# A transformer block with attention and routed experts on one core: GpSimd takes two elementwise steps from VectorE, its constants made between them

## The chip, the cores and the metric

The kernel runs on one core of a Trainium2 chip. The metric is the device time of one execution in microseconds (us). In the rows PE is TensorE (PEld its weight load), DVE is VectorE, ACT is ScalarE, POOL is GpSimd, SP is SyncE, which only issues DMAs; SPq and POOLq are the DMA-issuing sides of SP and POOL.

## What is computed

The input x holds 2 batches of 1024 tokens of 256 numbers. The result is x plus causal attention (16 heads of 16) plus a mixture of 8 experts (the 2 best for each token), both computed from the normalised rows:

```python
xn = _layernorm(x)
q, k, v = xn @ Wq + bq, xn @ Wk + bk, xn @ Wv + bv        # for each head
probs = softmax(causal(q @ k.T * HD ** -0.5))
attn = (probs @ v) @ Wo + bo
top, sel = top_k(xn @ Wr, 2);  w = softmax(top)
ffn = sum_e w_e * ((clip(silu(xn @ Wg[e]), -7, 7) * (xn @ Wu[e])) @ Wd[e])
out = x + attn + ffn
```

## The kernel before

Five instruction streams, one for each engine, walk one list, `PLAN`, made by `make_plan()`. Its entries are stages such as `("qk_lo", 3)`. Each engine has a table from stage names to its own functions (`walk`), skips the stages it has no function for, and executes the others strictly in the list's order. Semaphores tie the engines together, so a wait at the head of one engine's stream holds everything that stands behind it on that engine.

**Start.** Four quarters of 512 tokens: VectorE takes the variance (`"stats"`), GpSimd the inverse deviation (`inverse_deviation`, L555), VectorE normalises the rows (L743), TensorE transposes them (L936) and multiplies them by the q and k weights (L943).

**q and k in three parts.** The products are kept as a sum of three bf16 numbers, so that the scores can be made in bf16. For chunk k (128 x 512) ScalarE rounds the product and the bias to the first part (`qk_hi_part`, L640), VectorE subtracts it from the product (`qk_resid_part`, L752), ScalarE rounds the rest to the second part (`qk_mid_part`, L646), and VectorE subtracts again to get the third part (`qk_lo_part`, L760). SyncE stores each pair of chunks, 3 DMAs of 256 KB (`store`, L464), once all six parts are there, and loads the heads of a unit from the stored parts (`load`, L478). Chunks 0 to 7 (the first batch) are made at the start, chunks 8 to 15 (the second) in slots 0 to 24 of the main loop.

**GpSimd's constants.** Its stream begins with the masks, counters and ones that others need. One of them, `ones_row` (L572), is awaited by SyncE (`consts` at 4) before the DMA of ones into `packk` (L537), and behind that DMA stands all that SyncE issues later: the stores of the normalised rows (`store_xn`, L527), `store`, `load`.

**Routing.** VectorE finds the two best experts and a slot in the expert-sorted list for each token. GpSimd writes the list with 32 indirect DMAs, two for each group i of 128 tokens (`place_tokens(i)`, stage `"list"`, L595). SyncE loads the finished list (`load_list`, L505), VectorE makes token numbers of it (`token_of_slot`, L899 and L900), GpSimd gathers the rows (L604), and 39 expert tiles follow.

**Main loop.** 8 units of 4 heads in 12 steps g, each of 5 slots: four slots make scores and exponentials (TensorE L1028, ScalarE L668), the fifth multiplies by v (`weigh_v`, L1047). On diagonal steps GpSimd zeroes the upper triangle (`mask`, L620), and `weigh_v` waits for it. Beside them run the row maxima of the next unit (TensorE L1003, VectorE L788 and L791: a ring of three PSUM banks, so TensorE waits when VectorE stands still) and the experts' stages. The plan puts `("qk", 8 + k)` in slot 3k + 1 and `("qk_lo", 8 + k)` in slot 3k + 2 or one or two later, `("list", i)` for i of 4 and up at 2.5 slots each from slot 0, `("token",)` in slot 36, `("residual", t)` in slot 30 + 3t. The residual stage adds the output bias to x (`add_bias_to_x`, L775), 16 times 128 x 256; from slot 210 on others read its result.

Of the kernel before, what the change touches and what calls it, by code (L numbers as in the profile page):

```python
# [101 lines left out]
def stored(k, part):  # L102

    return part if qk_tile(k)[2] else PARTS - 1 - part
# [166 lines left out]
def build(nc, x_d, wqk_d, wvr_d, bqk_d, bv_d, wo_d, bo_d, wgu_d, wd_d, out_d):  # L271
    with ExitStack() as ctx:
# [272 lines left out]
        def _(pool):  # L545
# [7 lines left out]
            def inverse_deviation(q):  # L553
# [4 lines left out]
            pool.memset(padv[:, :], PAD).then_inc(consts, 1)  # L558
            chain(pool.memset(neghalf[:, :], -0.5))
            chain(pool.memset(ident[:, :], 0.0))  # L560
            chain(pool.affine_select(out=ident[:, :], in_=ident[:, :], compare_op=ALU.not_equal, fill=1.0, base=0,
                                     pattern=[[-1, P]], channel_multiplier=1))
            pool.tensor_copy(identb[:, :], ident[:, :]).then_inc(consts, 1)
            inverse_deviation(0)

            chain(pool.memset(maskrow[:, :], 0.0))
            pool.affine_select(out=maskrow[:, BANK - P:], in_=maskrow[:, BANK - P:], compare_op=ALU.is_ge, fill=NEG,
                               base=0, pattern=[[-1, P]], channel_multiplier=1).then_inc(consts, 1)
            inverse_deviation(1)
# [5 lines left out]
            chain(pool.memset(lower[:, :], 0.0))  # L575
            pool.affine_select(out=lower[:, :], in_=lower[:, :], compare_op=ALU.is_ge, fill=1.0, base=0,
                               pattern=[[-1, P]], channel_multiplier=1).then_inc(consts, 1)
            inverse_deviation(2)
            pool.memset(one8[:, :], 1.0)
            pool.iota(iota8[:, :], pattern=[[1, E]], base=0, channel_multiplier=0, allow_small_or_imprecise_dtypes=True)  # L580
            pool.iota(iota128[:, :], pattern=[[P, NT]], base=0, channel_multiplier=0,
                      allow_small_or_imprecise_dtypes=True)
            inverse_deviation(3)
# [136 lines left out]
        def _(dve):  # L720
# [450 lines left out]
```

## Time and profile before

| | before |
|---|---|
| median of 3 runs | 528.88 us (527.51 to 530.34) |
| the profiled execution, its own time | 527.32 us |
| its span, first to last instruction | 525.3 us |
| mean granted TensorE clock | 0.961 |
| busy: PE / DVE / ACT / POOL | 450.0 / 332.4 / 263.8 / 159.6 us |

The profile shows one execution. Busy time is the sum of an engine's instructions; what sets the end is better read from the chain of work that ended last, which names at each moment the instruction that the rest was waiting for. A granted clock of 1.0 is TensorE's 2.4 GHz, 0.5 is 1.2 GHz.

### The profile page before, as it was taken

The numbers are of one execution on the slowest core, as the hardware profiler recorded it, in microseconds if no ns is written. First come the engines' busy times: TensorE is split into PE (matmuls) and PEld (weight loads), VectorE is DVE, ScalarE is ACT, GpSimd is POOL, SyncE is SP. The second block draws the span as 40 slices with busy tenths as digits, with TensorE's granted clock in tenths as the row PEclk, the third lists the DMA queues.
The fourth block names the chain that finished last, engine by engine and source line by source line (L and its number), as shares of the span: only waits on it lengthen the run. The fifth ranks groups of instructions, "written<-read, shape, count | busy, mean of one in ns | idle before, by whom it ended". The sixth has DMA issues, their size and how long they took to land.

```text
span 525.3 us, 7823 instructions
## 1 busy us (share of the span) xinstructions
PE 450.0 (86%) x2368; PEld 203.5 (39%) x2368; DVE 332.4 (63%) x1023; ACT 263.8 (50%) x646; POOL 159.6 (30%) x198
## 2 busy tenths in 40 slices
PE   1777936987999999999989998899899989998876
PEld 1335612332344344434434444433433343433323
DVE  4585889785867686566665565546655666661671
ACT  1353300665446555564655454554555565656751
POOL 2210007584343233314341242123241333323020
PEclk9998965999799999999999999999999999999997
DMA  7469912587181008101810044001710101100851
GB/s 252 145 131 287 175 30 58 165 281 217 39 153 38 24 23 160 33 22 32 149 40 22 21 90 85 20 21 41 140 42 21 36 26 33 31 12 8 269 167 40
DMA packets 31726, 46.98 MB, mean 89 GB/s; under 512 B 6336, under 2 KB 18753, under 8 KB 31687
## 3 DMA queue, kind: packets, MB, share of 16 engines
q1 hardware_dynamic: 26055, 35.97, 27.9%
q0 software_dynamic: 4768, 9.33, 6.5%
q10 hardware_dynamic: 864, 1.19, 0.8%
q8 instruction: 20, 0.33, 0.3%
q14 instruction: 19, 0.16, 0.1%
HBM read 31.49 MB, written 15.63 MB: 90 GB/s over the span
## 4 chain that ended last, share of the span: by engine, by line
PE 65%; DVE 12%; ACT 7%; issue 6%; POOL 4%; DMA 4%; SPq 1%; POOLq 0%; ACTq 0%
PE ps_w L1085 14%; PE ps_y L1047 12%; PE ps_s L1028 9%; PE ps_s L1003 9%; PE ps_w L1113 7%; POOL slot_values L595 4%; ACT probs L668 4%; PE ps_w L1073 3%; PE ps_w L943 2%; DVE ps_s L788 2%; PE ps_w L967 2%; PE ps_w L1106 2%; DMA packk<-qk_parts 2%; PE ps_w L1080 1%; DVE mxa L791 1%
## 5 line engine op out<-in xcount | busy, mean ns | idle before, releaser
L668 ACT ACTIVATE probs<-ps_s 128x512 f32<-128x512 f32 (+3 forms) x384 | 176.9, 495 | 113.3 <-PE ps_s L1028 112.2
L788 DVE CUSTOM_DVE_ANT_0 ps_s<-ps_s,maskrow 128x128 f32<-128x128 f32 (+3 forms) x256 | 124.7, 500 | 59.6 <-PE ps_s L1003 58.6
L1003 PE MATMUL ps_s<-packk,packq 96*128 96x512 bf16 (+3 forms) x384 | 125.7, 344 | 18.6 <-DVE mxa L791 10.4
L1028 PE MATMUL ps_s<-packq,packk 99*128 99x512 bf16 (+3 forms) x384 | 121.4, 334 | 6.8 <-ACT probs L668 5.2
L791 DVE TENSOR_REDUCE mxa<-ps_s 128x1 f32<-128x512 f32 x128 | 88.2, 689 | 55.9 <-PE ps_s L1003 54.5
L1085 PE MATMUL ps_w<-wgu,xgt 128*128 x156 | 82.8, 613 | 3.3 <-issue 2.0
L1047 PE MATMUL ps_y<-probs,v 128*32 128x512 f32 (+3 forms) x768 | 82.7, 502 | 2.3 <-ACT probs L668 1.6
L610 POOL DMA_INDIRECT expert_rows<-yo,slots x39 | 39.6, 1015 | 125.7 <-ACT yo L706 123.4
L620 POOL TENSOR_SCALAR_AFFINE_SELECT probs<-probs 128x512 f32<-128x512 f32 x64 | 41.9, 654 | 112.0 <-ACT probs L668 111.6
L1028 PEld LDWEIGHTS ps_s<-packq,packk 99*128 99x128 bf16 x384 | 36.6, 98 | 91.6 <-ACT probs L668 55.0
L1003 PEld LDWEIGHTS ps_s<-packk,packq 96*128 96x128 bf16 x384 | 38.3, 100 | 64.0 <-issue 19.3
L604 POOL DMA_INDIRECT xg<-xn_rows,token x39 | 37.9, 972 | 34.6 <-PE ps_w L1080 23.0
L595 POOL DMA_INDIRECT slot_values<-slot_val,pos x32 | 32.1, 1002 | 53.0 <-DVE pos L884 44.1
L1113 PE MATMUL ps_w<-xnt,hidt 128*128 x156 | 41.6, 389 | 2.9 <-DVE y L821 2.4
L943 PE MATMUL ps_w<-xnt,wqk 128*128 128x512 f32 x64 | 33.8, 646 | 3.3 <-ACT xnt L630 1.9
L1085 PEld LDWEIGHTS ps_w<-wgu,xgt 128*128 128x128 f32 x156 | 25.8, 189 | 21.6 <-issue 18.4
L1113 PEld LDWEIGHTS ps_w<-xnt,hidt 128*128 128x128 f32 x156 | 27.8, 189 | 12.2 <-issue 7.4
L694 ACT ACTIVATE tanh<-ps_w 128x256 f32<-128x256 f32 x39 | 15.0, 384 | 33.9 <-PE ps_w L1085 33.9
L1047 PEld LDWEIGHTS ps_y<-probs,v 128*32 128x32 f32 x768 | 15.3, 108 | 39.8 <-ACT probs L668 22.3
L706 ACT ACTIVATE yo<-ps_w 128x256 f32<-128x256 f32 x39 | 15.0, 384 | 27.0 <-PE ps_w L1113 27.0
L907 DVE SCALAR_TENSOR_TENSOR tanh<-tanh,ps_w 128x256 f32<-128x256 f32 x39 | 16.2, 416 | 11.0 <-ACT tanh L694 10.9
L1073 PE MATMUL ps_w<-wo,yt 128*128 128x256 f32 x64 | 19.4, 429 | 4.3 <-ACT yt L681 2.3
(107 smaller groups left out, 395.0 us busy)
## 6 DMA issues: line engine op xcount, KB each, us to landing
qk_parts<-stage SPq DMA_DIRECT2D x24, 256.0 KB, 3.4
wgu<-in_wgu SPq DMA_DIRECT2D x8, 512.0 KB
stage<-expert_rows SPq DMA_DIRECT2D x16, 256.0 KB, 3.8
packq<-qk_parts SPq DMA_DIRECT2D x8, 384.0 KB, 5.3
packk<-qk_parts SPq DMA_DIRECT2D x8, 384.0 KB, 7.2
x<-in_x SPq DMA_DIRECT2D x4, 512.0 KB, 8.5
xn_rows<-probs SPq DMA_DIRECT2D x4, 512.0 KB, 9.2
packq<-qk_parts SPq DMA_DIRECT2D x8, 256.0 KB, 7.9
```

Of the source, the lines that this page charges most:

```text
L595: pool.indirect_dma_start(out=slot_d, out_offset=bass.IndirectOffsetOnAxis(ap=pos[:, k, i:i + 1], axis=0), in_=slot_val[:, i, k:k + 1], in ...
L610: pool.indirect_dma_start(out=z_d, out_offset=bass.IndirectOffsetOnAxis(ap=slots[:, i:i + 1], axis=0), in_=yo[:, i % 2, :], in_offset=None ...
L620: pool.affine_select(out=cols, in_=cols, compare_op=ALU.is_ge, fill=0.0, base=0, pattern=[[0, UH], [1, P]], channel_multiplier=-1).then_in ...
L668: act.activation(probs[:, g % 2, h, 0:width], ps_s[:, score_bank(k), 0:width], ACT.Exp, scale=SCALE)\
L788: ins = dve.tensor_tensor_reduce(out=chunk, in0=chunk, in1=maskrow[:, BANK - width:], scale=1.0, scalar=NEG, op0=ALU.add, op1=ALU.max, acc ...
L791: ins = dve.tensor_reduce(into, chunk, op=ALU.max, axis=AX.X)
L943: return pe.matmul(ps_w[:, bank, :], wqk[:, op, c, P * grp:P * (grp + 1)], xnt_moe[:, c, cols], start=c == 0, stop=c == DC - 1)
L1003: pe.matmul(ps_s[:, SCORE_RING + n % NAT_RING, 0:width], packq[0:MAXROW, u % SLOTS, h, P * i:P * (i + 1)], packk[0:MAXROW, u % SLOTS, h, B ...
L1028: pe.matmul(ps_s[:, score_bank(k), 0:width], packk[0:KROWS, u % SLOTS, h, P * j:P * (j + 1)], packq[0:KROWS, u % SLOTS, h, t0:t0 + width], ...
L1047: ins = pe.matmul(ps_y[32 * h:32 * h + 32, t0 - BANK * c:BANK], v[:, TB * b + j, at:at + 32], probs[:, g % 2, h, 0:width], start=j == 0, s ...
L1085: return pe.matmul(ps_w[:, bank, :], xgt[:, i % 2, c, :], wgu[:, bass.ds(expert[i] * (DC * 2 * F) + c * 2 * F, 2 * F)], start=c == 0, stop ...
L1113: ins = pe.matmul(ps_w[:, bank, 0:D], hidt[:, i % 2, c, :], wd[:, bass.ds(expert[i] * (DC * D) + c * D, D)], start=c == 0, stop=c == DC - 1)
```

## The change

`qk_lo_part` and `add_bias_to_x` move from VectorE's table to GpSimd's, at the same places of the plan. GpSimd's constants, so far written in one piece ahead of its walk, are cut in four functions that are called at the stages `("stats", 0)` to `("stats", 3)`. In the third, the memset of `ones_row` also waits for `qk_lo` at 2.

```diff
-            pool.wait_ge(rstd_ready, 2)
-            pool.memset(ones_row[MAXROW:KROWS, :], 1.0).then_inc(consts, 1)
-            pool.wait_ge(consts, 4)
...
+            def triangle():
+
+                pool.wait_ge(rstd_ready, 2)
+                pool.wait_ge(qk_lo, 2)
+                pool.memset(ones_row[MAXROW:KROWS, :], 1.0).then_inc(consts, 1)
+                pool.wait_ge(consts, 4)
...
+            def prepare(q):
+                (first_constants, mask_and_ones, triangle, counters)[q]()
...
-            walk({"list": place_tokens, "gather": gather, "scatter": scatter, "s": mask})
+            def qk_lo_part(k):
+                w, op = divmod(k, 2)
+                cols = slice(BANK * op, BANK * (op + 1))
+                pool.wait_ge(qk_mid, k + 1)
+                pool.tensor_tensor(stage[:, w % 2, stored(k, 2), cols], resid[:, k % 2, :], stage[:, w % 2, stored(k, 1), cols],
+                                  ALU.subtract).then_inc(qk_lo, 1)
+
+            def add_bias_to_x(t):
+                wait_freed(pool, ("bias",))
+                pool.tensor_tensor(x[:, t, :], x[:, t, :], bo[:, :], ALU.add).then_inc(residual_ready, 1)
+
+            walk({"stats": prepare, "qk_lo": qk_lo_part, "residual": add_bias_to_x, "list": place_tokens, "gather": gather,
+                  "scatter": scatter, "s": mask})
...
-            def qk_lo_part(k):
-                w, op = divmod(k, 2)
-                cols = slice(BANK * op, BANK * (op + 1))
-                dve.wait_ge(qk_mid, k + 1)
-                dve.tensor_tensor(stage[:, w % 2, stored(k, 2), cols], resid[:, k % 2, :], stage[:, w % 2, stored(k, 1), cols],
-                                  ALU.subtract).then_inc(qk_lo, 1)
...
-            def add_bias_to_x(t):
-                wait_freed(dve, ("bias",))
-                dve.tensor_tensor(x[:, t, :], x[:, t, :], bo[:, :], ALU.add).then_inc(residual_ready, 1)
```

**GpSimd's order at the start, of before.** The stream from the second inverse deviation (`rstd`) on; the memset of `wgu` is `ones_row`.

```order
L555 TENSOR_TENSOR rstd<-vareps,neghalf 128x4 [waits var_ready]
L572 MEMSET wgu 3x1024 [waits rstd_ready]
L575 MEMSET lower 128x128 [waits consts]
L576 AFFINE_SELECT lower<-lower 128x128 [waits const_step]
L555 TENSOR_TENSOR rstd<-vareps,neghalf 128x4 [waits var_ready]
```

The same place, of the changed kernel.

```order
L555 TENSOR_TENSOR rstd<-vareps,neghalf 128x4 [waits var_ready]
L638 TENSOR_TENSOR stage<-resid,stage 128x512 [waits qk_mid] x2
L579 MEMSET wgu 3x1024 [waits qk_lo,rstd_ready]
L581 MEMSET lower 128x128 [waits consts]
L582 AFFINE_SELECT lower<-lower 128x128 [waits const_step]
L555 TENSOR_TENSOR rstd<-vareps,neghalf 128x4 [waits var_ready]
L638 TENSOR_TENSOR stage<-resid,stage 128x512 [waits qk_mid] x2
```

Two third parts now stand ahead of `ones_row`, and two more behind the third inverse deviation.

**GpSimd's order in slots 0 to 40 of the main loop, of before.** The DMAs to `slot_values` write the list, AFFINE_SELECT is the mask of one step, the DMAs to `xg` are the first gathers.

```order
L595 DMA slot_values<-slot_val,pos 4992x1 [waits list_init,pos_ready]
L595 DMA slot_values<-slot_val,pos 4992x1 x11
L620 AFFINE_SELECT probs<-probs 128x4x128 [waits probs_ready]
L595 DMA slot_values<-slot_val,pos 4992x1 x4
L620 AFFINE_SELECT probs<-probs 128x4x128 [waits probs_ready]
L595 DMA slot_values<-slot_val,pos 4992x1 x4
L620 AFFINE_SELECT probs<-probs 128x4x128 [waits probs_ready]
L595 DMA slot_values<-slot_val,pos 4992x1 x4
L620 AFFINE_SELECT probs<-probs 128x4x128 [waits probs_ready]
L595 DMA slot_values<-slot_val,pos 4992x1 x8
L604 DMA xg<-xn_rows,token 128x256 [waits xn_out,token_ready]
```

The same place, of the changed kernel, up to the third mask; behind it four more third parts stand among the last 12 list DMAs, and three bias additions behind the last of these.

```order
L606 DMA slot_values<-slot_val,pos 4992x1 [waits list_init,pos_ready]
L606 DMA slot_values<-slot_val,pos 4992x1 x9
L638 TENSOR_TENSOR stage<-resid,stage 128x512 [waits qk_mid]
L606 DMA slot_values<-slot_val,pos 4992x1 x2
L631 AFFINE_SELECT probs<-probs 128x4x128 [waits probs_ready]
L638 TENSOR_TENSOR stage<-resid,stage 128x512 [waits qk_mid]
L606 DMA slot_values<-slot_val,pos 4992x1 x4
L631 AFFINE_SELECT probs<-probs 128x4x128 [waits probs_ready]
L638 TENSOR_TENSOR stage<-resid,stage 128x512 [waits qk_mid]
L606 DMA slot_values<-slot_val,pos 4992x1 x2
L638 TENSOR_TENSOR stage<-resid,stage 128x512 [waits qk_mid]
L606 DMA slot_values<-slot_val,pos 4992x1 x2
```

Eight third parts now stand between the tenth list DMA and the last, the first of them ahead of the first mask.

## Rows read from the trace of the kernel before

**Rows 1.** The page, chain that ended last: its shares by engine.

```profile
PE 65%; DVE 12%; ACT 7%; issue 6%; POOL 4%; DMA 4%; SPq 1%; POOLq 0%; ACTq 0%
```

**Rows 2.** The chain in order of time, start: start us, us, what.

```profile
28.54 0.70 DVE stage L760
...
30.36 2.62 DMA qk_parts<-stage
...
35.34 9.58 DMA packk<-qk_parts
```

**Rows 3.** Timeline of SP's DMA issues, start: start us, us, instruction.

```profile
15.08 0.94 SPq L537 DMA_DIRECT2D packk<-wgu  x1
...
16.51 3.74 SPq L527 DMA_DIRECT2D xn_rows<-probs  x1
...
22.43 8.43 SPq L464 DMA_DIRECT2D qk_parts<-stage  x6
```

**Rows 4.** Windows: us, busy of PE PEld DVE ACT POOL, PEclk, DMA share, GB/s.

```profile
18.50:21.00 2.50, 1.51 (x7) 0.53 (x5) 1.55 (x3) 1.23 (x4) 0.00 (x0) 1.00 0.26 46
...
31.00:32.00 1.00, 1.00 (x4) 0.52 (x3) 0.93 (x8) 0.00 (x0) 0.00 (x0) 1.00 1.01 340
```

**Rows 5.** Timeline of ScalarE and GpSimd, start, and ScalarE at chunk 8.

```profile
20.06 0.61 ACT L646 CAST stage<-resid 128x512 bf16<-128x512 f32 x1
20.98 0.62 ACT L646 CAST stage<-resid 128x512 bf16<-128x512 f32 x1 [0.31 <-DVE resid L752]
...
14.11 0.95 POOL L572 MEMSET wgu<- 3x1024 bf16 x1
...
95.43 0.62 ACT L646 CAST stage<-resid 128x512 bf16<-128x512 f32 x1 [0.33 <-DVE resid L752]
```

**Rows 6.** Instruction groups of POOL and DVE: busy, mean ns, idle before.

```profile
L620 POOL TENSOR_SCALAR_AFFINE_SELECT probs<-probs 128x512 f32<-128x512 f32 x64 | 41.9, 654 | 112.0 <-ACT probs L668 111.6
...
L561 POOL TENSOR_SCALAR_AFFINE_SELECT ident<-ident 128x128 f32<-128x128 f32 x1 | 0.3, 286 | 0.2 <-POOL ident L560 0.2
...
L760 DVE TENSOR_TENSOR stage<-resid,stage 128x512 bf16<-128x512 f32 x16 | 11.5, 723 | 2.5 <-ACT stage L646 1.9
...
L775 DVE TENSOR_TENSOR x<-x,bo 128x256 f32<-128x256 f32 x16 | 6.9, 431 | 0.0
```

**Rows 7.** The chain in order of time, end of the list.

```profile
124.13 4.08 DMA slot_values<-slot_val,pos
128.22 1.79 DMA slots<-slot_values
...
130.25 0.18 DVE token L900
```

**Rows 8.** Timeline of GpSimd among the list DMAs, and its wait behind them.

```profile
91.90 0.96 POOL L595 DMA_INDIRECT slot_values<-slot_val,pos  x1 [0.30 <-issue]
96.62 0.65 POOL L620 TENSOR_SCALAR_AFFINE_SELECT probs<-probs 128x512 f32<-128x512 f32 x1 [3.76 <-ACT probs L668]
...
108.61 1.23 POOL L595 DMA_INDIRECT slot_values<-slot_val,pos  x1 [0.17 <-issue]
...
117.62 1.16 POOL L595 DMA_INDIRECT slot_values<-slot_val,pos  x1 [0.30 <-issue]
...
130.71 0.98 POOL L604 DMA_INDIRECT xg<-xn_rows,token  x1 [5.62 <-DVE token L900]
```

**Rows 9.** Timeline of VectorE beside the first of these long list DMAs.

```profile
108.05 0.95 DVE L760 TENSOR_TENSOR stage<-resid,stage 128x512 bf16<-128x512 f32 x1 [0.68 <-ACT stage L646]
```

**Rows 10.** Waits from 126 to 135 us: who waited for whom, us, times, longest.

```profile
PE ps_s L1003 <- DVE mxa L788: 3.3, 1, 3.3
```

**Rows 11.** Timeline of SP, the experts' down weights.

```profile
119.63 3.83 SPq L501 DMA_DIRECT2D xnt<-in_wd  x6
```

**Rows 12.** The chain in order of time, a bias addition in it.

```profile
143.38 0.28 DVE x L775
```

**Rows 13.** Window behind the wait for the list, columns as in rows 4.

```profile
130.00:140.00 10.00, 8.85 (x37) 2.66 (x38) 7.72 (x26) 3.71 (x8) 4.15 (x5) 0.66 0.25 71
```

More of the change, by code:

```diff
@@ L556, in inverse_deviation @@
                     .then_inc(rstd_ready, 1)
[L558 to L569, printed above, removed]
-            pool.wait_ge(rstd_ready, 2)
-            pool.memset(ones_row[MAXROW:KROWS, :], 1.0).then_inc(consts, 1)
-            pool.wait_ge(consts, 4)
-            chain(pool.memset(lower[:, :], 0.0))
@@ L576, in _ @@
[L576 to L582, printed above, removed]
@@ L583, in _, with first_constants @@
-            inverse_deviation(3)
-            pool.iota(iota_t[:, :], pattern=[[1, MAX_TILES]], base=0, channel_multiplier=0,
-                      allow_small_or_imprecise_dtypes=True)
-            pool.iota(slot_val[:, :, :], pattern=[[2 * P, NT], [1, 2]], base=0, channel_multiplier=2).then_inc(consts, 1)
-            pool.memset(ones[:, :], 1.0).then_inc(consts, 1)
+            def first_constants():
+                pool.memset(padv[:, :], PAD).then_inc(consts, 1)
+                chain(pool.memset(neghalf[:, :], -0.5))
+                chain(pool.memset(ident[:, :], 0.0))
+                chain(pool.affine_select(out=ident[:, :], in_=ident[:, :], compare_op=ALU.not_equal, fill=1.0, base=0,
+                                         pattern=[[-1, P]], channel_multiplier=1))
+                pool.tensor_copy(identb[:, :], ident[:, :]).then_inc(consts, 1)
+                inverse_deviation(0)
@@ new lines, in mask_and_ones @@
+            def mask_and_ones():
+                chain(pool.memset(maskrow[:, :], 0.0))
+                pool.affine_select(out=maskrow[:, BANK - P:], in_=maskrow[:, BANK - P:], compare_op=ALU.is_ge, fill=NEG,
+                                   base=0, pattern=[[-1, P]], channel_multiplier=1).then_inc(consts, 1)
+                inverse_deviation(1)
+            def triangle():
[3 more added lines that the diff above has]
+                pool.wait_ge(consts, 4)
+                chain(pool.memset(lower[:, :], 0.0))
+                pool.affine_select(out=lower[:, :], in_=lower[:, :], compare_op=ALU.is_ge, fill=1.0, base=0,
+                                   pattern=[[-1, P]], channel_multiplier=1).then_inc(consts, 1)
+                inverse_deviation(2)
@@ new lines, in counters @@
+            def counters():
+                pool.memset(one8[:, :], 1.0)
+                pool.iota(iota8[:, :], pattern=[[1, E]], base=0, channel_multiplier=0, allow_small_or_imprecise_dtypes=True)
+                pool.iota(iota128[:, :], pattern=[[P, NT]], base=0, channel_multiplier=0,
+                          allow_small_or_imprecise_dtypes=True)
+                inverse_deviation(3)
+                pool.iota(iota_t[:, :], pattern=[[1, MAX_TILES]], base=0, channel_multiplier=0,
+                          allow_small_or_imprecise_dtypes=True)
+                pool.iota(slot_val[:, :, :], pattern=[[2 * P, NT], [1, 2]], base=0, channel_multiplier=2).then_inc(consts, 1)
+                pool.memset(ones[:, :], 1.0).then_inc(consts, 1)
@@ L918, in first_constants @@
                     widen_v_bias()
-            walk({"stats": variance, "ln": normalise_rows, "qk": qk_resid_part, "qk_lo": qk_lo_part,
+            walk({"stats": variance, "ln": normalise_rows, "qk": qk_resid_part,
                   "store": first_constants, "top": best_two, "place": place_slots, "token": token_of_slot,
-                  "bias": add_bias, "residual": add_bias_to_x, "nat": row_max, "negate": negate_max, "neg": copy_neg,
+                  "bias": add_bias, "nat": row_max, "negate": negate_max, "neg": copy_neg,
                   "norm": normalise, "moe_hid": hidden, "sum": add_experts, "proj": add_projection})
```

## The prediction, made before the changed kernel had run

> **What bounds the kernel now.** I read first the chain that ended last, by engine: TensorE has 65% of it, VectorE 12%, GpSimd only 4% [rows 1]. So work taken from VectorE is worth little on the average, and the question is where the chain runs through the work that changes hands or through GpSimd. The chain in order of time answers it: there are two such places.
>
> The first is the start. The chain passes the third part of chunk 3 on VectorE (28.54 to 29.24), the store behind it (last DMA issued at 30.36, landed at 32.98) and the load of the first heads (landed at 44.92) [rows 2]; TensorE has nothing to do before that load is in. The second is the list. Its last DMA starts at 124.13 and lands 4.08 us later, the list is loaded in 1.79, and the token numbers are made at 130.25 [rows 7]. VectorE waits for the list in its own stream, so its row maxima stop, and TensorE stands idle for 3.3 us behind them [rows 10]. Ahead of this GpSimd runs from 96.62 to the end of the list with no wait longer than the gaps of about 0.3 us between its DMAs [rows 8]: what is added to its stream there arrives later at everybody.
>
> **What GpSimd needs for a third part.** No row shows a GpSimd subtraction of this size. From below, its mask reads one input of 128 x 512 f32 and takes 654 ns; its 128 x 128 form takes 286 [rows 6]. So 384 more elements cost 368 ns, 0.96 ns each, over a fixed 0.16 us. From above I take twice the mask, 1.31 us, as two inputs of that size must pass. I choose t = 0.16 + 2 x 512 x 0.00096 = 1.15 us, near the upper end because the operation does read two tensors; VectorE needs 0.72 [rows 6]. A bias addition, half as long, comes to 0.65 us by the same sum, against 0.43 on VectorE.
>
> **The change at the start.** The second parts of chunks 0 and 1 end at 20.67 and 21.60 [rows 5], so the third parts on GpSimd run 20.7 to 21.9 and 21.9 to 23.05; VectorE had them done before the store was issued at 22.43 [rows 3]. The store itself would be 0.7 us late. But `ones_row` now waits for both: 0.95 us of memset [rows 5] brings it to 24.1, and SyncE stands at that wait with everything behind it. Its DMA of ones was issued at 15.08, so it moves by 9.0 us, and the two stores of normalised rows, which used to go out in a gap, move with it. The second of these took 3.74 us to issue, until 20.25 [rows 3], and the 16 DMA engines were only 26% busy, at 46 GB/s, while it stood there [rows 4]. I read that as the slow little DMA of ones in front of it, and it keeps its place in front. Issuing of ones and rows took 20.25 - 15.08 = 5.17 us, so SyncE comes to the first store at 24.1 + 5.17 = 29.3 instead of 22.43, 6.9 us late. The second store could not go before 29.24 in the old order either, so the loss is mostly made up; what is left is data. At 340 GB/s [rows 4] the second 512 KB of rows need 1.5 us and the two stores (six times 256 KB) 4.6 us. From 29.3 plus about 0.9 us until data flows and is confirmed that gives 36.3, against 32.98: **+3.3 us**. The load of 9.58 us behind it starts as much later, and TensorE, idle already, waits as much longer. The bounds: 0.7 us, if the long issue was not due to the ones (then only the slower third parts are seen), and 6.9 us, if the second store keeps its distance from the first. VectorE's own relief here buys nothing, since the chain passes it once, and GpSimd takes over exactly that piece.
>
> **The change in the list.** The first third part of the second batch, chunk 8, can't start before its second part is ready, at 95.43 + 0.62 = 96.05 [rows 5]. Before, GpSimd filled that time with list DMAs 11 and 12 (90.64 to 92.86: 0.96, a gap of 0.30, 0.96) and then waited 3.76 us for the exponentials [rows 8]. Now it waits with only ten done, runs the third part, then the two DMAs (2.22 us), and comes to the first mask at 96.05 + 0.1 + t + 0.2 + 2.2 = 99.7 for t = 1.15, where it was at 96.62. So the cover of 3.76 us is used up by waiting, not by the new work: +3.05. The other seven fall in the stretch without cover. Four stand behind a mask and cost t each, three between two DMAs, where they replace about 0.13 us of the gap. That is 7 x 1.15 - 3 x 0.13 = 7.7 us. In all +10.7 us.
>
> One thing is given back. Four list DMAs took 1.16 to 1.31 us instead of 0.96, the first at 108.61 and the last at 117.62 [rows 8], and each began while a third part ran on VectorE, as at 108.05 [rows 9]. Without these the four save 0.27 + 0.34 + 0.27 + 0.20 = 1.1 us: the list ends **9.6 us** later, or 0.4 + 8t. The Trainium skill, SBUF — State Buffer, section "Who interferes with whom", has it that a VectorE instruction with two SBUF inputs and a GpSimd instruction that reads SBUF exclude each other for its whole length. By that rule the 1.1 us are gained in full, since nothing with two SBUF inputs is left on VectorE here; without it the DMAs would stay as long as they were, and the sum would be 10.7.
>
> Behind GpSimd wait its masks, and for each of them TensorE's product with v: the second to fourth mask come about 5, 7 and 9 us later than before, so TensorE, full until now, gets idle time there. All of it lies ahead of the list's end and is not added to it: from the fourth mask to the token numbers TensorE has as much to do as before, while GpSimd has two third parts more. ScalarE and VectorE fall back with it, because the chunk after next waits for a third part. The stores of the last chunks, and behind them on SyncE the six loads of down weights that went out from 119.63 to 123.46 [rows 11], move nearer to the last list DMAs, so these share the DMA engines with more data at the end: an estimate of +0.5 (bounds 0 and 1.5, what 0.5 MB take at 340 GB/s).
>
> **The bias additions.** Three run on GpSimd between the last list DMA and the first gather, where it waited 5.62 us [rows 8]: 2.0 us, covered. If that cover were gone they would delay the first gather by 2.0. The other 13 lie among masks, gathers and scatters after 133 us, where GpSimd is busy 4.15 of 10 us [rows 13]. 8.5 us spread over 30 fit. VectorE saves 16 x 0.43 = 6.9 us, but such a piece stands only twice in the chain, with 0.28 us each (one of them in [rows 12]): **-0.5 us**.
>
> **The sum.** 3.3 + 9.6 + 0.5 - 0.5 = +12.9 us. The profiled execution's own time, 527.32, goes to 540.2; it lies 1.6 below the median of the runs, so for the median I say 528.9 + 12.9 = 541.8.
>
> **Rivals.**
> 1. *Heavier: the clock falls once or twice more.* Behind the idle 3.3 us the granted clock of ten microseconds was 0.66 [rows 13], so TensorE ran at half speed for 6.8 of them and lost 3.4 us. The new waits behind late masks may bring that about again, before the list's end. Against it: there TensorE is not the one waited for. Once to three times, with more of the start's upper bound: 545 to 552.
> 2. *Lighter: GpSimd is nearer to its one-input rate, or the late rows cost nothing at the start.* t = 0.65 makes the list 0.4 + 5.2 = 5.6 instead of 9.6, a gain of 4.0 and 0.5 more in the start; a start of 0.7 gives 2.6. Either or both: 534 to 539.
> 3. *Not slower: VectorE's relief outruns the delay.* The place is every wait of TensorE on the row maxima from 96 to 162 us and the start. All 32 instructions taken from VectorE are 11.5 + 6.9 = 18.4 us [rows 6]. If each one shortened the chain, the time would be 528.9 + 13.4 - 18.4 = 524; it decides once 13.4 of the 18.4 us lie on the chain. The profile speaks against it: in the chain they are 0.7 once and 0.28 twice.
>
> **How the numbers follow.** My forecast, 539 to 545, gets 0.60, the heavier case 0.15, the lighter 0.20, the third 0.05. The range that leaves out no more than 2 in 10 goes from 534 to 549: lighter than 534 or heavier than 549 is left out. 0.5%, 2.6 us, is about what a measurement of this kernel can tell from no change. The first three cases are all slower by more than that, 0.95; of the third I give 0.03 to faster, and 0.02 to a relief that just balances.
>
> **What would show it.** At the start: the DMA of ones issued at about 24, the first store at about 29, the load of the first heads landed at about 48 instead of 44.92. Third parts of about 1.15 us on GpSimd. The list's last DMA some 13 us later, list DMAs of 0.96 without the long ones, TensorE's idle time ahead of the token numbers longer, at 5 to 6 us. From there to the end the same length as before. The prediction is wrong if the third parts are far from 1.15 us, if SyncE's long issue doesn't recur behind the ones, or if the stretch behind the token numbers gets shorter, which would mean that VectorE was holding TensorE there.

## The result, and the profile after

The changed kernel took 544.75 us in the median of 4 runs (543.68 to 546.01), the kernel before 528.21 on the same chip (4 runs, 527.51 to 530.34). The ratio is 1.031 (95% interval 1.027 to 1.035): slower by 16.5 us. The forecast was 541.8, between 534 and 549. Ratios are of the fast runs alone, without those more than 1.5% above the fastest of the same kernel: among others one of 864 us in e12, one of 598 of the kernel before, and seven of its 17 runs on the second chip, which puts the ratios there 0.4 to 0.5% above those of the medians.

The page of the changed kernel, first its span and the busy time of each engine, then the chain that ended last, and the third parts, which are new on GpSimd (busy, mean ns of one, idle before):

```profile
span 542.0 us, 7824 instructions
...
PE 453.0 (84%) x2368; PEld 205.5 (38%) x2368; DVE 320.3 (59%) x991; ACT 263.9 (49%) x646; POOL 187.9 (35%) x230
...
PE 61%; DVE 11%; POOL 7%; ACT 7%; issue 6%; DMA 5%; SPq 2%; POOLq 0%; ACTq 0%
...
L638 POOL TENSOR_TENSOR stage<-resid,stage 128x512 bf16<-128x512 f32 x16 | 18.6, 1172 | 25.4 <-ACT stage L669 25.3
```

GpSimd's share of the chain goes from 4% [rows 1] to 7%, though it is busy for only 35% of the span. The two places named ahead of the run show where. Line numbers of the changed kernel are higher: L638 is the third part on GpSimd, L606 the list DMA, L631 the mask, L643 the bias addition, L912 the token numbers.

**The start.** SyncE's issues, to be read against [rows 3] (start us, us it took to issue them, instruction):

```profile
25.09 0.93 SPq L537 DMA_DIRECT2D packk<-wgu  x1
26.07 4.18 SPq L527 DMA_DIRECT2D xn_rows<-probs  x2
30.37 5.84 SPq L464 DMA_DIRECT2D qk_parts<-stage  x6
...
41.08 0.43 SPq L478 DMA_DIRECT2D packk<-qk_parts  x1
```

The ones moved from 15.08 to 25.09 us and everything behind them in the queue moved too; the first store goes out at 30.37 instead of 22.43. The chain in order of time says why they moved, and ends in TensorE's first score product at 50.50, which was at 44.96:

```profile
20.45 0.69 ACT stage L663
21.14 0.52 ACT stage L669
...
21.72 2.28 POOL stage L638 x2
...
24.12 0.96 POOL wgu L579
...
26.50 3.74 SPq L527
...
35.53 3.19 DMA qk_parts<-stage
...
41.08 9.38 DMA packk<-qk_parts
```

Two third parts on GpSimd, then the memset of the ones (its destination has the name `wgu`, whose space it shares), then SyncE, which stands for 3.74 us at the second store of normalised rows, then the stores. **+5.5 us** at this point.

**The list.** GpSimd's timeline at the first mask of the main loop, against [rows 8]:

```profile
94.89 0.95 POOL L606 DMA_INDIRECT slot_values<-slot_val,pos  x1 [0.30 <-issue]
101.60 1.16 POOL L638 TENSOR_TENSOR stage<-resid,stage 128x512 bf16<-128x512 f32 x1 [5.76 <-ACT stage L669]
102.91 0.99 POOL L606 DMA_INDIRECT slot_values<-slot_val,pos  x1 [0.15 <-issue]
104.20 0.96 POOL L606 DMA_INDIRECT slot_values<-slot_val,pos  x1 [0.30 <-issue]
105.17 0.65 POOL L631 TENSOR_SCALAR_AFFINE_SELECT probs<-probs 128x512 f32<-128x512 f32 x1
105.79 1.16 POOL L638 TENSOR_TENSOR stage<-resid,stage 128x512 bf16<-128x512 f32 x1
```

GpSimd waits 5.76 us for chunk 8's second part with ten list DMAs done, and only then makes the third part and the two DMAs that used to fill that wait. From the first list DMA (83.26) to the last (139.36) it is now 56.10 us; before it was 46.39 (77.74 to 124.13). **+9.7 us.** The chain behind the last one, against [rows 7]:

```profile
139.36 5.95 DMA slot_values<-slot_val,pos
...
145.33 1.80 DMA slots<-slot_values
...
147.37 0.18 DVE token L912
...
148.27 0.61 PE ps_s L1015
```

The last DMA takes 5.95 us to land instead of 4.08: **+1.9 us**. The token numbers are 17.1 us late. The timelines of TensorE and VectorE tell who waits there, TensorE for 7.15 us where it was 3.3 [rows 10] and 5 to 6 were forecast:

```profile
148.27 0.61 PE L1015 MATMUL ps_s<-packk,packq 96*128 96x512 bf16 x1 [7.15 <-DVE mxa L800]
```

```profile
147.15 0.18 DVE L911 TENSOR_SCALAR clip<-slots 128x39 int32<-128x39 int32 x1 [8.37 <-DMA slots<-slot_values]
```

**Behind the token numbers** the kernel takes 394.63 us, before 395.05: **-0.4 us**. The sum is 5.5 + 9.7 + 1.9 - 0.4 = 16.7, the difference of the spans (542.0 - 525.3). It compares one execution of each kernel; the experiments show that each of the four terms moves by about 1 us, up to 1.4, from one execution to the next.

### The profile page after: what moved, and what is told of

Its sections match the earlier page's. It is cut to its first block, busy times and chain, and to the rows that moved or that the text cites. A ratio compares the mean times of both kernels' runs of the same rounds, so it can differ in the third digit from the quotient of the medians.

```text
span 542.0 us, 7824 instructions
## 1 busy us (share of the span) xinstructions
PE 453.0 (84%) x2368; PEld 205.5 (38%) x2368; DVE 320.3 (59%) x991; ACT 263.9 (49%) x646; POOL 187.9 (35%) x230
## 4 chain that ended last, share of the span: by engine, by line
PE 61%; DVE 11%; POOL 7%; ACT 7%; issue 6%; DMA 5%; SPq 2%; POOLq 0%; ACTq 0%
PE ps_w L1097 13%; PE ps_y L1059 11%; PE ps_s L1040 9%; PE ps_s L1015 8%; PE ps_w L1125 7%; POOL slot_values L606 4%; ACT probs L691 4%; PE ps_w L1085 3%; POOL stage L638 2%; PE ps_w L1118 2%; PE ps_w L979 2%; DVE ps_s L800 2%; DMA packk<-qk_parts 2%; PE ps_w L955 2%; PE ps_w L1092 1%
## 5 line engine op out<-in xcount | busy, mean ns | idle before, releaser
L1059 PE MATMUL ps_y<-probs,v 128*32 128x512 f32 (+3 forms) x768 | 82.7, 502 | 10.4 <-POOL probs L631 8.6
L631 POOL TENSOR_SCALAR_AFFINE_SELECT probs<-probs 128x512 f32<-128x512 f32 x64 | 41.5, 649 | 103.4 <-ACT probs L691 103.1
L1040 PEld LDWEIGHTS ps_s<-packq,packk 99*128 99x128 bf16 x384 | 36.7, 98 | 89.9 <-ACT probs L691 52.5
L606 POOL DMA_INDIRECT slot_values<-slot_val,pos x32 | 31.1, 973 | 43.5 <-DVE pos L896 35.1
L955 PE MATMUL ps_w<-xnt,wqk 128*128 128x512 f32 x64 | 37.5, 707 | 6.5 <-DVE resid L775 4.5
L1097 PEld LDWEIGHTS ps_w<-wgu,xgt 128*128 128x128 f32 x156 | 25.8, 189 | 21.6 <-issue 18.4
L638 POOL TENSOR_TENSOR stage<-resid,stage 128x512 bf16<-128x512 f32 x16 | 18.6, 1172 | 25.4 <-ACT stage L669 25.3
L775 DVE SCALAR_TENSOR_TENSOR resid<-ps_w,bqk,stage 128x512 f32<-128x512 f32 x16 | 11.9, 750 | 25.7 <-ACT stage L663 22.3
```

The costliest lines, as they stand in the source:

```text
L606: pool.indirect_dma_start(out=slot_d, out_offset=bass.IndirectOffsetOnAxis(ap=pos[:, k, i:i + 1], axis=0), in_=slot_val[:, i, k:k + 1], in ...
L631: pool.affine_select(out=cols, in_=cols, compare_op=ALU.is_ge, fill=0.0, base=0, pattern=[[0, UH], [1, P]], channel_multiplier=-1).then_in ...
L955: return pe.matmul(ps_w[:, bank, :], wqk[:, op, c, P * grp:P * (grp + 1)], xnt_moe[:, c, cols], start=c == 0, stop=c == DC - 1)
L1040: pe.matmul(ps_s[:, score_bank(k), 0:width], packk[0:KROWS, u % SLOTS, h, P * j:P * (j + 1)], packq[0:KROWS, u % SLOTS, h, t0:t0 + width], ...
L1059: ins = pe.matmul(ps_y[32 * h:32 * h + 32, t0 - BANK * c:BANK], v[:, TB * b + j, at:at + 32], probs[:, g % 2, h, 0:width], start=j == 0, s ...
L1097: return pe.matmul(ps_w[:, bank, :], xgt[:, i % 2, c, :], wgu[:, bass.ds(expert[i] * (DC * 2 * F) + c * 2 * F, 2 * F)], start=c == 0, stop ...
```

## The experiments

Twelve experiments ran on three other chips; one of them is the kernel before once more, and one a repetition. The kernel before took 534.99 us on the second chip (17 runs, 527.4 to 537.2), 528.02 on the third (23 runs) and 531.05 on the fourth (29 runs). Since these differ by more than some of the effects, I read each profile by the same marks as above. A profile is one execution, and often one of the shortest: e2's own time was 537.0 where the median is 541.1, e4's 531.4 where it is 536.3. The marks are TensorE's first score product, the length from the first list DMA to the last, the landing of the last, the token numbers, and what follows them. In us:

| kernel | first score product | list, first to last | landing | token at | behind it | span |
|---|---|---|---|---|---|---|
| before | 44.96 | 46.39 | 4.09 | 130.25 | 395.05 | 525.3 |
| after | 50.50 | 56.10 | 5.97 | 147.37 | 394.63 | 542.0 |
| e1, ones early | 46.21 | 56.87 | 6.13 | 144.84 | 393.26 | 538.1 |
| e9, ones behind the load | 47.13 | 56.06 | 6.46 | 144.20 | 395.50 | 539.7 |
| e2, first batch alone | 49.12 | 47.83 | 5.72 | 140.60 | 394.20 | 534.8 |
| e3, second batch alone | 44.20 | 56.94 | 5.73 | 140.33 | 394.57 | 534.9 |
| e4, bias alone | 44.96 | 48.46 | 4.76 | 134.72 | 394.68 | 529.4 |
| e4b, the same again | 45.34 | 47.59 | 4.45 | 132.38 | 394.02 | 526.4 |
| b_again, before again | 44.43 | 46.76 | 5.09 | 131.05 | 394.65 | 525.7 |
| e5, down weights behind the list | 49.98 | 57.03 | 2.17 | 144.93 | 395.37 | 540.3 |
| e11, ones early and e5 | 45.86 | 56.79 | 2.17 | 140.16 | 395.44 | 535.6 |
| e6, list further ahead | 44.98 | 44.96 | 5.72 | 129.20 | 395.00 | 524.2 |
| e10, e6 and e5 on before | 44.71 | 48.56 | 2.17 | 130.87 | 395.23 | 526.1 |
| e12, e10 and bias | 45.60 | 48.57 | 2.17 | 131.59 | 393.31 | 524.9 |

("Landing" runs from the start of the last list DMA to the issue of the list's load.)

**e1: is it the order in SyncE's queue?** The changed kernel, with the ones made ahead of the third parts again:

```diff
                 inverse_deviation(1)
+                pool.wait_ge(rstd_ready, 2)
+                pool.memset(ones_row[MAXROW:KROWS, :], 1.0).then_inc(consts, 1)
+                pool.wait_ge(consts, 4)
...
-                pool.wait_ge(rstd_ready, 2)
-                pool.wait_ge(qk_lo, 2)
-                pool.memset(ones_row[MAXROW:KROWS, :], 1.0).then_inc(consts, 1)
```

> The changed kernel with one thing undone: ones_row is set ahead of the first third parts, as before, so SyncE is not held. Theory A (the start is lost by SyncE's order: the DMA of ones and the two stores of rows pushed into the stores of q and k): the DMA of ones is issued at about 15 us again, the load of the first heads lands at 46 instead of 50.5, and the time is 544.8 - 4.5 = 540. Theory B (the start is lost by the slower third parts themselves, or by TensorE's slow first products): the load still lands at 49 to 50 and the time stays at 543.5 to 545.

It took 540.88 us, 1.015 of the kernel before beside it (1.010 to 1.021), which was itself 7 us longer on this chip than on the first; this holds for the next two as well, and the marks in the table are the better witness. The first score product came at 46.21, 4.3 us earlier than in the changed kernel and 1.25 later than before. So most of the start's loss is the wait for the ones; the third parts on GpSimd themselves, with the other constants at their new places, cost about 1 us. Of the 4.3 us, 2.5 reach the token numbers. Behind these the code is the changed kernel's, and yet it takes 1.4 us less (393.26 for 394.63): that much of the column is scatter.

**e2: the first batch alone.** The changed kernel, with the third parts of chunks 8 to 15 and the bias additions back on VectorE (the first function of the diff is GpSimd's, the second VectorE's):

```diff
 def qk_lo_part(k):
+    if k >= 8:
+        return
...
+def qk_lo_part(k):
+    if k < 8:
+        return
```

> Only the first batch's third parts (chunks 0 to 7) and the cut-up constants on GpSimd; the second batch's third parts and the bias additions stay on VectorE. If the start and the list add up as separate costs: the start's 5.5 us alone, 528.2 + 5.5 = 533.7, with the list's stretch as long as before (first list DMA to token numbers 52.5 us). If they interact (the late start is partly soaked up later): 530 to 532.

541.09 us (ratio 1.016, 1.010 to 1.022). The start is late as in the changed kernel (49.12), and the list is back at 47.83 us. The rest of the expectation missed: the span is 9.5 us above the first profile's, not 5.5, and from the first list DMA to the token numbers it took 57.9 us, not 52.5. The landing was 5.72, and VectorE did not wait for the list: it was loaded at 139.0, the numbers were made at 140.60, because TensorE was behind. TensorE had stood still for 2.38 us up to 123.47 and for 1.80 up to 128.77, with no releaser named. The cause of these waits is open.

**e3: the second batch alone.** The kernel before, with the third parts of chunks 8 to 15 on GpSimd (the same edit, the other way round):

> The kernel before with only the second batch's third parts (chunks 8 to 15) on GpSimd. Theory A (eight subtractions lengthen the stretch in which GpSimd writes the list, about 0.4 + 8 x 1.16 = 9.7 us, and the down weights then delay the list's landing by 1.9): 528.2 + 11.6 = 539.8. Theory B (the list's stretch has cover, and most of the loss came with the late start): below 534.

539.34 us (ratio 1.012, 1.007 to 1.018). The start is untouched, the list 56.94 us: +10.55 from eight third parts and nothing else. The token numbers are at 140.33, +10.1, and the span is 9.6 us longer, where 11.6 were expected. e2's start and e3's list put the two large terms where the prediction had them; the two spans don't add up to the changed kernel's (9.5 + 9.6 against 16.7), since e2's holds the unexplained waits. GpSimd's timeline shows the price of one, and that most list DMAs beside them keep their 0.96 to 0.99:

```profile
117.00 1.16 POOL L631 TENSOR_TENSOR stage<-resid,stage 128x512 bf16<-128x512 f32 x1
118.33 0.98 POOL L595 DMA_INDIRECT slot_values<-slot_val,pos  x1 [0.17 <-issue]
119.61 0.96 POOL L595 DMA_INDIRECT slot_values<-slot_val,pos  x1 [0.30 <-issue]
```

**e4 and e4b: the bias additions alone.** The kernel before, with only this edit:

```diff
+def add_bias_to_x(t):
+    wait_freed(pool, ("bias",))
+    pool.tensor_tensor(x[:, t, :], x[:, t, :], bo[:, :], ALU.add).then_inc(residual_ready, 1)
```

> The kernel before with only the 16 bias additions on GpSimd, no constants moved. Theory A (covered by GpSimd's idle time, VectorE's relief hardly on the chain): 527.2 to 528.7, -1.0 to +0.5. Theory B (they delay the first gathers and masks): 529.5 to 531. Theory C (VectorE was holding TensorE there): 521 to 525.

> The kernel before with the additions of the output bias on GpSimd alone, a second time: on the second chip it took 536.3 us beside 535.0 of a kernel before that was itself 7 us longer there than on the others. Theory (GpSimd's 8 free us behind the list cover them, VectorE is spared 0.4 us each time): within 1 us of the kernel before, the part from the token to the end 0 to 0.5 us shorter, the token where it was. Rival (they stand in front of masks and row transfers on GpSimd and make those late): 1.5 us or more longer, with the part behind the token over 396 us.

The first time 536.29 us (ratio to before 1.007, 1.003 to 1.011), the second 532.25 (1.001, 0.998 to 1.005). Behind the token numbers the two took 394.68 and 394.02 us, against 395.05 and 394.65 in the two profiles of the kernel before: a few tenths, the sign of the forecast -0.5, but less than the 1.4 us of scatter in this column. So the additions cost nothing that can be seen, and that they gain 0.5 is not shown. The first run alone would have said 3.8 us slower by the ratio, 1.3 by the medians. Its token numbers are 4.5 us late: 1.6 of it was there at the first mask (98.21), after the stall at 91 to 97 us (last section) and ahead of any bias addition; 1.1 came up to the list's load, and 1.8 behind it, where VectorE made the numbers late without waiting for the list. The second run has the first mask as late (98.04) and the numbers only 2.1 us late. The three additions behind the last list DMA end well inside GpSimd's wait:

```profile
127.12 2.10 POOL L625 TENSOR_TENSOR x<-x,bo 128x256 f32<-128x256 f32 x3
135.18 0.98 POOL L604 DMA_INDIRECT xg<-xn_rows,token  x1 [5.96 <-DVE token L900]
```

**b_again: the kernel before, once more.**

> The kernel before, unchanged, profiled once more on the chip of the runs beside it. On the second chip the kernel before took 527 to 537 us over 17 runs, on the first 527.5 to 530.3. Theory: the whole difference between 528 and 535 lies ahead of the first token, in the stretch from the first to the last mask (46.4 us in the first profile), with a lower granted clock of TensorE there, and the part from the token to the end stays at 394 to 395 us. Rival: it is spread over the whole span; then the part behind the token is over 397 us.

528.56 us, the ratio to the kernel before beside it 1.002 (1.000 to 1.004). So this chip is like the first, and the 535 us of the second chip were not met again; the theory on where they come from was not tested. Two executions of the same kernel differ by 1.0 us in the landing, 0.5 at the first score product and 0.4 in the list, and e1 above by 1.4 behind the token numbers: smaller differences in the table mean nothing.

**e9: the same question as e1, from the other side.** Third parts first, then the ones, as in the changed kernel; but SyncE issues the ones behind the first load:

```diff
-            sp.wait_ge(consts, 4)
-            sp.dma_start(packk[MAXROW:KROWS, :, :, :].rearrange("p s h t -> p (s h) t"),
...
+                if u == 0:
+                    sp.wait_ge(consts, 4)
+                    sp.dma_start(packk[MAXROW:KROWS, :, :, :].rearrange("p s h t -> p (s h) t"),
```

> The kernel after, but the transfer of the ones is issued behind the first load of the packed parts instead of ahead of the first stores; the ones are still written behind GpSimd's third parts. Theory (the wait for the ones holds SyncE's queue, and stores and loads stand behind it): first store at about 22 to 23 us instead of 30.4, the load's last issue at about 36.5 instead of 41.1, TensorE's first score matmul at about 46 to 47 instead of 50.5, as where the ones were written first (46.2), and the whole about 4 us shorter than after. Rival (the third parts on GpSimd make the stores late by themselves): first score matmul still above 49 us and less than 1.5 us gained. The second store of x's transpose took 3.74 us to issue behind the ones; if the ones ahead of it were the cause, it now takes about 0.5 us.

541.41 us, ratio 1.026 (1.023 to 1.029) where the changed kernel has 1.031 (1.027 to 1.035); the intervals overlap, so it is the mark that tells. The first score product is at 47.13, 3.4 us earlier. Its issues:

```profile
15.54 0.36 SPq L531 DMA_DIRECT2D xn_rows<-probs  x1
24.12 8.34 SPq L464 DMA_DIRECT2D qk_parts<-stage  x6
...
37.91 0.94 SPq L482 DMA_DIRECT2D packk<-wgu  x1
38.90 0.39 SPq L531 DMA_DIRECT2D xn_rows<-probs  x1
39.41 4.07 SPq L464 DMA_DIRECT2D qk_parts<-stage  x3
```

The second store of normalised rows (15.54), which took 3.74 us, now takes 0.36, as the first at 11.09 does. The slow issue has gone to the DMAs behind the ones: the third store of rows takes 0.39, the three stores of parts behind it 0.49, 1.31 and 2.18, 4.07 in all. So the slow issue does follow the little DMA of ones (3 partitions), as the prediction had read it, though here it falls on the third and fourth DMA behind it and not on the second. Such issues also occur without it: in the kernel before one store at 42.40 took 2.73 us. In e1, where the ones go first at 14.92, the two stores of rows take 4.11 us again:

```profile
14.92 0.94 SPq L537 DMA_DIRECT2D packk<-wgu  x1
15.90 4.11 SPq L527 DMA_DIRECT2D xn_rows<-probs  x2
23.22 8.28 SPq L464 DMA_DIRECT2D qk_parts<-stage  x6
```

**e5: what makes the last list DMA land late?** The changed kernel, with the loads of the down weights planned behind the list's load:

```diff
-        at(8 * QK_GAP + 3 + k, ("wd", k))
+        at(LIST_TO + 3 + k // 2, ("wd", k))
```

> The kernel after, but the first down weights are loaded behind the list's load instead of just ahead of it. Theory (they share the DMA engines with the last transfer of the list): the list's last transfer lands in about 4 us instead of 5.95, the token comes 1.9 us earlier, the end as much, 542.9 for 544.75. Rival 1 (the landing is longer because of the stores of the attention output or its own descriptor work): still 5.5 to 6 us, no gain. Rival 2: the down weights are late for the first expert tile, and what is won ahead of the token is lost behind it: the part behind the token grows from 394.6 to 396 or more.

542.03 us, ratio 1.026 (1.023 to 1.029): 2.5 us less than the changed kernel by the ratios, whose intervals overlap. The landing is 2.17 us, not the expected 4:

```profile
140.88 2.15 DMA slot_values<-slot_val,pos
```

The loads were part of this wait in the kernel before as well (4.09 and 5.09 in its two profiles). In the changed kernel the engines carried 349 GB/s while everybody waited (window: us, busy of PE, PEld, DVE, ACT, POOL, granted clock, DMA share, GB/s), where e5 had 12:

```profile
142.00:145.00 3.00, 0.00 (x0) 0.00 (x0) 0.00 (x0) 0.00 (x0) 0.42 (x1) 1.00 0.94 349
```

```profile
142.00:145.00 3.00, 0.11 (x1) 0.00 (x0) 0.26 (x2) 0.96 (x2) 1.95 (x3) 0.97 0.08 12
```

How long the landing takes goes with how late the sixth load is issued. It went out 1.1 us ahead of the last list DMA in the kernel before (landing 4.09), 0.8 ahead in b_again (5.09), together with it in e6 (5.72), and 0.4 behind it in the changed kernel (5.97). Of the 3.8 us won in the landing 2.4 reach the token numbers; the list itself ended 1.5 us later in this execution. Behind them it took 0.7 us more than in the changed kernel (395.37), which could be the later weights, or scatter.

**e11: both repairs.** The changed kernel with the edits of e1 and e5.

> The kernel after with two repairs: the ones written ahead of the third parts, and the down weights loaded behind the list. Theory (the terms of the prediction add up): 544.75 less 4.2 for the start and 2.5 to 3.5 for the list's landing, 537 to 538 us; what stays over the kernel before is GpSimd's eight third parts among the list, +9.7 us. Rival (each hides the other): above 539.5 us, no better than either repair alone (540.9 and 542.0).

538.20 us (536.4 to 539.8), ratio 1.014 (1.010 to 1.018), beside a kernel before at 531.05. The two add up: the start is at 45.86, the landing 2.17, the token numbers at 140.16. What remains over the first profile of the kernel before, 10.3 us of span, is +0.9 for the start, +0.7 up to the first list DMA, +10.4 for the list, -1.9 for the landing, -0.1 up to the token numbers and +0.4 behind them. Its span is 6.4 us shorter than the changed kernel's.

**e6, e10, e12: can the kernel before be made faster by the same knowledge?** One more step of the list ahead of the first mask:

```diff
-LIST_EARLY, LIST_TO = 4, 6 * SPS
+LIST_EARLY, LIST_TO = 5, 6 * SPS
```

> The kernel before, but the list runs five steps ahead of the first mask instead of four, which puts two more of its 32 transfers ahead of it. Theory (GpSimd's own order from the first mask to the last transfer bounds the token): 2 transfers of 1.0 us fewer in the stretch, 44.3 us instead of 46.4, and the time 1 to 2 us shorter if TensorE's side is no later. Rival: TensorE's products with the values end as late as the list, or the two transfers make the first mask late by as much: within 0.5 us of the kernel before.

526.57 us, ratio 0.9975 (0.995 to 1.000). The list takes 44.96 us, 1.4 to 1.8 less, and the token numbers come 1.1 to 1.9 us earlier. It is the best version found, by 1.4 us, at the edge of what can be told from nothing. Its landing is 5.72 us, since the down weights now go out together with the last list DMA. e10 adds the edit of e5 to it, e12 that of e4 as well:

> The kernel before with the list one step further ahead and the first down weights loaded behind the list instead of ahead of its last transfer. Theory: the list's last transfer lands in 2.2 us, as where the weights were moved in the changed kernel, instead of 4.1 to 5.7; with the earlier list the token comes 3 to 4.5 us earlier than in the kernel before, about 524 us in all. Rival 1: TensorE's score products, not the list, are then late for VectorE's turn to make the token, and half or more of it is not had: 526 to 527 us. Rival 2: the down weights are late for the first expert tile and what is won is lost behind the token (part behind the token 396 us or more).

> The kernel beside it (list one step further ahead, down weights behind it) with the additions of the output bias on GpSimd as well. Theory: the additions are worth 0 to 0.5 us once the token is no longer late: 523.5 to 524 us, the same as its neighbour within the scatter. Rival (with a shorter wait behind the list, 3.6 us instead of 5.6 us of cover, the three additions there end after the token and hold up the first row transfer): 1 us or more longer than its neighbour.

529.72 us (ratio 0.999, 0.996 to 1.002) and 529.29 (0.997, 0.993 to 1.0005), beside 531.05: no gain that can be told from nothing, and no loss by the bias additions; the 524 us expected of e10 and the 523.5 to 524 of e12 were missed by 5 us. The landing is 2.17 as expected, but the token numbers of e10 were not waited for. It had its list loaded at 129.9, and made the numbers only at 130.87, with no wait for the load: VectorE's row maxima and TensorE were as late. That is rival 1 in the measured time; yet TensorE was late at least in part by a stall at 91 to 97 us (the first mask is at 100.22) and not by its own work, so this profile doesn't say what the two edits give where it doesn't stall.

## Why the prediction was right, and where its terms were off

**The list: right in mechanism and size.** 9.6 us were forecast, 9.7 measured. The six kernels with eight third parts in the list have 56.1 to 57.0 us of it, the two profiles of the kernel before 46.4 and 46.8, so the term lies between 9.3 and 10.6, and that it was met to 0.1 is in part luck. t was chosen as 1.15 us between 0.65 and 1.31; it is 1.17. The first mask was to be at 99.7 if the start had not moved; it is at 105.17 with a start 5.5 us late, which is 99.7. The next three masks were to be 5, 7 and 9 us late; beyond the start they are 4.2, 6.4 and 8.0. GpSimd's cover of 3.76 us was indeed used up by waiting: eight third parts cost a bit more than 8t because the first of them also holds two list DMAs back.

The 1.1 us given back by shorter list DMAs also came: of the list DMAs in the kernel before five took over 1.1 us, in the changed kernel one. All fourteen profiles together say what the long ones have in common. Without the first of each profile, which always takes 1.22 us, 38 list DMAs started while a third part or a bias addition ran on VectorE: 25 of them took 1.16 to 1.48 us, 13 took 0.96 to 1.01. Of the other 396 none took more than 0.99. This agrees with the rule of the Trainium skill, SBUF — State Buffer, "Who interferes with whom", that a VectorE instruction with two SBUF inputs contends with a GpSimd instruction that reads SBUF. It does not agree with what the same section infers of such an instruction, that it leaves GpSimd's descriptor generation alone; here the measurement decides.

The forecast passed over the price the other way. In the changed kernel VectorE's four normalisations took 3.05 us while two third parts ran on GpSimd:

```profile
38.83 3.05 DVE L766 TENSOR_SCALAR probs<-x,mv,rstd 128x256 f32<-128x256 f32 x4
```

```profile
38.99 2.42 POOL L638 TENSOR_TENSOR stage<-resid,stage 128x512 bf16<-128x512 f32 x2 [5.47 <-ACT stage L669]
```

In the kernel before four of them took 1.38 us. One by one, the first and the last took 0.40 here too, and the second and third, which overlap a third part each, 1.25 and 1.24. The Trainium skill, SBUF — State Buffer, "Who interferes with whom", says that of a VectorE operation in a mode with two ports and a GpSimd instruction the one that is issued first has the shared port pair for its whole length, and the other is blocked. The two long normalisations fit that: each ends about 0.15 us behind a third part (40.40 behind 40.25, 41.55 behind 41.40). In which mode they ran no run shows. Here it cost nothing that the marks show, since TensorE waited for the load of the first heads until 50.50.

**The start: right in mechanism, 0.9 to 2.2 us too small.** The three profiles with the changed kernel's start have the first score product 5.5 us (this one), 5.0 (e5) and 4.2 (e2) behind the first profile of the kernel before; 3.3 were forecast. "From 29.3 plus about 0.9 us ... that gives 36.3, against 32.98: +3.3". SyncE's part went as said: ones and rows took 30.37 - 25.09 = 5.28 us to issue (5.17 forecast). Two things were mis-sized. The ones went out at 25.09 instead of 24.1, because the second parts were 1.0 us late: TensorE's first eight products took 6.47 us, and 5.46 before. e9 has it too (6.42); e1, e2 and e11 don't (5.65, 5.22, 5.19), and e5 lies between (5.96). e2 and e5 have the changed kernel's code up to there, so it changes from one execution to the next; why, no run shows. And the rows and the six stores, priced at 340 GB/s, took 8.35 us from the first store's issue (30.37) to the last landing (35.53 + 3.19 = 38.72), against 7.0 forecast (36.3 - 29.3). The engines carried less than I had assumed, 267 GB/s from 30.4 to 38.7 us, and 291 in the middle of it (columns as in rows 4):

```profile
33.00:36.00 3.00, 0.76 (x2) 0.00 (x0) 0.15 (x1) 0.00 (x0) 0.51 (x4) 1.00 0.85 291
```

The first of these is at least in part scatter, the second the mis-sized term. The measured 5.5 lies inside the bounds of 0.7 and 6.9. The condition of the lower bound, that the long issue is not due to the ones, was not met.

**The down weights: right in direction, too small.** 0.5 us was forecast within 0 to 1.5, and 1.9 measured against the first profile of the kernel before. Against b_again, which landed in 5.09, it is 0.9: the term is known to about 1 us only. "What 0.5 MB take at 340 GB/s" was the weak step. Six loads of 256 KB, 1.5 MB, were issued from 137.05 to 140.2, in the same 3 us as the last list DMAs, and e5 shows what they cost in all: 3.8 us of 5.97. The 4.08 us of [rows 7] already held some 2 us of them, and what was to be forecast was how much nearer the loads come to the last list DMA.

**The bias additions: not contradicted, not shown.** -0.5 forecast, -0.4 measured, inside the scatter of 1.4 us of the part behind the token numbers. One took 0.73 us on GpSimd, where 0.65 had been worked out. That they fit into GpSimd's idle time, e4b shows.

**The clock.** The heavier rival had it fall once or twice more. Up to the token numbers it fell twice more. From 37 to 42 us, behind a wait of TensorE of 4.55 us that ended with the first stores, the granted clock was 0.50, that is 1.2 GHz, and in a stretch ahead of the list's end its mean was 0.72 of the full 2.4:

```profile
37.00:42.00 5.00, 3.69 (x5) 1.63 (x6) 4.37 (x6) 2.28 (x4) 2.42 (x2) 0.50 0.58 137
127.00:133.00 6.00, 4.72 (x23) 3.00 (x23) 2.26 (x7) 2.29 (x5) 5.13 (x6) 0.72 0.27 84
```

Ahead of the second TensorE had stood still for masks (3.6 us the longest time). Neither cost anything that the marks show: TensorE waited for the load of the first heads in the one place, and GpSimd was the one waited for in the other, as the case against the rival said.

**The sum.** 12.9 forecast, 16.7 in the profiles: start +2.2, landing +1.4, list +0.1, bias +0.1. The two large misses went the same way. The mis-sized part of both is the price of data behind other data: at the start I took 340 GB/s, the rate of a microsecond with the DMA engines full [rows 4], where the whole stretch had 267. About 1 us of the first miss and as much of the second is scatter between executions. The rival that ended faster was wrong where it was doubted: 18.4 us of VectorE's work went away, and the kernel became 16.5 us slower.

## What to carry to other kernels

Before work is given to an engine with idle time, look for the stretch in which that engine has none: GpSimd was busy 30% of the span before the change, and 9.7 of the 16.7 us lost come from the 46 in which its order sets the end. Count what a wait holds in a DMA queue, not only what it waits for: the 3-partition DMA of ones now waits for two third parts, which could not start before 21.7 us, and that moved the first store behind it by 7.9 us and the landing of the load behind the stores by 5.5. And a DMA that many wait for should be timed with the traffic that is issued just before it: moving weight loads behind it took 3.8 us off its landing, of which 2.4 reached those who waited.

## What the runs showed of the hardware that was not expected

- **The DMA of ones** (3 partitions) takes 0.94 us to issue itself, and DMAs behind it become slow to issue: the second for 3.74 us, with the DMA engines 26% busy [rows 4], or in e9 the third and fourth for 1.31 and 2.18. Why it is so was not tried.
- **The landing of the last list DMA** is 2.17 us with the weight loads moved behind it, the same in four kernels, and 4.1 to 6.5 us with these loads beside it.
- **A stall at 91 to 97 us** is there in some profiles and not in others. In b_again ScalarE's second exponential started at 92.48, in e10, whose code of TensorE, ScalarE and VectorE is the same up to there, at 94.71:

```profile
92.48 0.60 ACT L668 ACTIVATE probs<-ps_s 128x512 f32<-128x512 f32 x1 [1.69 <-PE ps_s L1028]
```

```profile
94.71 0.60 ACT L668 ACTIVATE probs<-ps_s 128x512 f32<-128x512 f32 x1 [3.65 <-issue]
97.53 0.69 ACT L640 ACTIVATE stage<-ps_w,bqk 128x512 bf16<-128x512 f32 x1 [2.22 <-remote]
```

VectorE stood still for 5.48 us at the same time, and the first mask came at 100.22 instead of 96.15. The profile of e10 names no releaser but "issue" and "remote". The expert weights were being loaded then, but from 91 to 93 us at 416 GB/s in e10 and at 414 in b_again, so that alone doesn't tell the two apart. e4, e4b and e12 have the same wait of ScalarE (3.8, 2.9 and 3.6 us), and e2 has 3.7, up to 99.94. Whether it comes by chance is open: each of the two kernels that were profiled twice has the same answer both times, the kernel before no stall, e4 and e4b a stall. It may be what made the kernel before 7 us longer on the second chip, but no profile of it was taken there: that stays open, and so does the cause of the stall.
